# Language-model layer on one core: the value products of a query block in two calls of two heads each

## The chip, the core and the metric

The kernel runs on one NeuronCore of a Trainium2 chip. Its engines are TensorE (PE, with weight loads shown as PEld), VectorE (DVE), ScalarE (ACT), GpSimd (POOL) and SyncE (SP), which work side by side and wait for one another on semaphores. The metric is the device time of one execution in microseconds, as the median of several runs; lower is better.

## The reference

A layer of a language model over 2 sequences of 1024 tokens, width 512, all in float32: an embedding (hot tokens from a table, the others from a smaller table times a projection), causal attention with 16 heads of 32 columns, and a mixture of 16 experts, two of them for each token, beside a shared expert. The change touches the attention:

```python
def _L0_attn_ref(x, w_project, w_out):        # x: layernorm of the embedding
    qkv = jnp.einsum('bsd,od->bso', x, w_project)
    ...
    att = jnp.einsum('bhqd,bhkd->bhqk', q, k) / math.sqrt(HEAD_DIM)
    att = jnp.where(causal[None, None, :, :], jnp.float32(-1000000000.0), att)
    att = jax.nn.softmax(att, axis=-1)
    out = jnp.einsum('bhqk,bhkd->bhqd', att, v)
    out = jnp.transpose(out, (0, 2, 1, 3)).reshape(b, s, d)
    return jnp.einsum('bsd,od->bso', out, w_out)
```

The products of `att` with `v` are the value products.

## The kernel before

The program runs the embedding, the attention and the experts one after another. Every engine has its own program, written out by hand in program order; semaphores (`s_...`) tie them together.

The attention works in eight *units* `u`: four groups `g` of four heads (`GH` = 4) times two sequences `b`. A unit has eight *blocks* `i` of 128 query rows, and a block has four *steps*, one for each head, so a unit has 32 steps `n`, with i = n // 4 and head h = n % 4. Block i sees i + 1 key tiles of 128.

For step n the work passes through the engines like this. TensorE makes the scores (`scores`, line 676). VectorE adds the mask and takes the row maximum (line 815). ScalarE takes the exponentials, unnormalised, into `probs` (line 773). TensorE transposes each 128-wide tile of `probs` into PSUM banks 4 and 5 (`turn`, line 686). ScalarE copies the first bank of a head, key tiles 0 to 3, to `probsT` (line 758, semaphore `s_Ca`), and VectorE the second, which blocks 4 to 7 have (line 760, `s_Cd`). When all four heads of a block are copied, TensorE makes the value products (`heads`, line 699): for each key tile j and head h, `v_unit` (128 x 32) stands in the array and `probsT` (128 x 128) moves through it; the result of head h adds up in partitions 32h to 32h + 31 of PSUM bank 6. A transpose of the reciprocal row sums into another part of bank 6 follows (line 702, `z_inv`) and raises `s_PV`. ScalarE copies that (line 780, `z_rows`), and VectorE multiplies bank 6 with it into `attnT` (line 830, `s_AT`), which frees the bank for the next block.

TensorE's queue in step n of a unit is, in this order: the scores of a later step (n + 2 in the first half of a unit, n + 1 in the second), the transposes of step n - 1, in most steps a piece of the projections of the next unit (`fill_piece`, lines 629 and 642), and, in steps with n % 4 == 2, the value products of the block before. That is two steps behind the end of that block: its last head is transposed in step n % 4 == 0 and copied while TensorE is in the step after. In a unit's first block (n = 2) they are those of block 7 of the unit before. The last unit has no projection pieces. Behind it the transposes of its last step, the first tile of the output projection (line 651) and the value products of the last block follow.

ScalarE goes through copy of step n - 2, exponentials of step n, and in steps with n % 4 == 3 the copy to `z_rows`; VectorE through the row maximum of step n, copy of step n - 2, in steps with n % 4 == 0 the reciprocals for `z_inv`, and with n % 4 == 3 the multiplication into `attnT`.

Of the kernel before, what the change touches and what calls it, by code (L numbers as in the profile page):

```python
# [28 lines left out]
GROUPS, GH = HEADS // 4, 4  # L29
ATT_SCALE = float(HD) ** -0.5  # L30
QT = SEQ // P
# [37 lines left out]
def build(nc, a, out):  # L69
    ctx = ExitStack()  # L70
    with ctx:
# [3 lines left out]
        def sem(name):  # L75
            return ctx.enter_context(nc.semaphore(name))
# [18 lines left out]
        def bank(i, n=1):  # L95
            return psum[:, i:i + n, :].rearrange("p a n -> p (a n)")
# [247 lines left out]
        s_AT = sem("attnT_ready")  # L344
# [44 lines left out]
        HEAD = 16  # L389
# [6 lines left out]
        def score_bank(n):  # L396
            return bank(n % 4) if n < NARROW else bank(2 * (n % 2), 2)

        def turned_banks(i):
            return 1 if i < 4 else 2  # L400
# [9 lines left out]
        def bank_no(i, h, k):  # L410
            return banks.index((i, h, k))

        def copies(e, upto):

            return sum(copier(*x) == e for x in banks[:upto])

        def wait_bank_free(pe, u, n):

            m = n - 2
            x = banks[m % UB]  # L420
            v = u if m >= 0 else u - 1
            e = copier(*x)
            pe.wait_ge(s_Ca if e == "act" else s_Cd, HEAD + v * UCOPY[e] + copies(e, m % UB + 1))
# [191 lines left out]
        def fill_piece(pe, u, b, f, k, loads):  # L615

            if k == 0:

                if f >= 4:
                    pe.wait_ge(s_w, loads)  # L620
                copied, count = ((s_fdve, 0), (s_fact, 1), (s_fdve, 1), (s_fact, 2), (s_fdve, 2), (s_fact, 3))[f]
                pe.wait_ge(copied, HEAD + 3 * u + count)
            if f < 4:
                side, half = f % 2, f // 2
                if side == 0:
                    pe.wait_ge(s_wqlo, 4 * (u // 2) + k + 1)
                    pe.wait_ge(s_xplo, 8 * (u - 1) + 4 * half + k + 1)
                for t, (w, x) in enumerate(((wq_hi, x_lo), (wq_hi, x_hi), (wq_lo, x_hi))):
                    mm = pe.matmul(bank(7), w[:, k, side * P:(side + 1) * P], x[:, k, :],  # L629
                                   start=(k == 0 and t == 0), stop=(k == KC - 1 and t == 2), skip_group_check=True)  # L630
                if side == 1 and k < KC - 1:
                    mm.then_inc(s_xpused, 1)
            else:
                mm = value_products(pe, b, f, k)
            if k == KC - 1:
                mm.then_inc(s_fill, 1)

        def value_products(pe, b, f, k):

            t0 = b * SEQ + ((f - 4) * 4 + k) * P  # L640
            for c in range(KC):
                mm = pe.matmul(bank(7)[:, k * P:(k + 1) * P], xnT[:, c, t0:t0 + P],  # L642
                               w_unit[:, c, 2 * P:3 * P], start=(c == 0), stop=(c == KC - 1))
            return mm

        def output_tile(pe, c):

            pe.wait_ge(s_atlo, c + 1)
            for g in range(GROUPS):
                for t, (x, w) in enumerate(((at_hi, wo_hi), (at_lo, wo_hi), (at_hi, wo_lo))):  # L650
                    mm = pe.matmul(bank(c % 2), x[:, c % 2, g * P:(g + 1) * P], w[:, g, :],  # L651
                                   start=(g == 0 and t == 0), stop=(g == GROUPS - 1 and t == 2))
            mm.then_inc(s_op, 1)

        def att_pe(pe):
            def scores(u, b, n):
                i, h = n // GH, n % GH

                if n < 2:
                    pe.wait_ge(s_E, HEAD + u * STEPS - 1)  # L660
                elif n < 4:
                    pe.wait_ge(s_E, HEAD + u * STEPS)
                elif n < NARROW:
                    pe.wait_ge(s_E, HEAD + u * STEPS + n - 3)
                elif n == NARROW:
                    pe.wait_ge(s_E, HEAD + u * STEPS + n - 2)
                else:
                    pe.wait_ge(s_E, HEAD + u * STEPS + n - 1)
                dst = score_bank(n)
                if n == NARROW:  # L670
                    pe.wait_ge(s_high[b], STACKED * (u // 2 + 1))
                qs = q_stack[:, h, i * P:(i + 1) * P]
                for c0, ks in ((0, k_low[b]), (512, k_high))[0:1 if n < NARROW else 2]:

                    c1 = min(max((i + 1) * P, c0 + 256), c0 + 512)
                    mm = pe.matmul(dst[:, c0:c1], qs, ks[:, h, 0:c1 - c0], start=True, stop=True)  # L676
                mm.then_inc(s_S, 1)

            def turn(u, n):
                i, h = n // GH, n % GH  # L680
                pe.wait_ge(s_E, HEAD + u * STEPS + n + 1)
                for k in range(turned_banks(i)):
                    m = bank_no(i, h, k)
                    wait_bank_free(pe, u, m)
                    for j in range(4 * k, min(4 * k + 4, i + 1)):
                        mm = pe.transpose(bank(4 + m % 2)[:, (j - 4 * k) * P:(j - 4 * k + 1) * P],  # L686
                                          probs[n % PSLOTS][:, j * P:(j + 1) * P], ident[:, :])
                    mm.then_inc(s_T, 1)

            def heads(u, b, i):  # L690

                last = bank_no(i, GH - 1, turned_banks(i) - 1) + 1
                for e, s in (("act", s_Ca), ("dve", s_Cd)):
                    pe.wait_ge(s, HEAD + u * UCOPY[e] + copies(e, last))

                pe.wait_ge(s_AT, HEAD + u * QT + i)
                for j in range(i + 1):
                    for h in range(GH):
                        pe.matmul(bank(6)[32 * h:32 * h + 32, 0:P], v_unit[b][:, j, 32 * h:32 * h + 32],  # L699
                                  probsT[i % 2][:, h, j * P:(j + 1) * P], start=(j == 0), stop=(j == i))  # L700
                pe.wait_ge(s_Z, HEAD + u * QT + i + 1)
                pe.transpose(bank(6)[:, P:2 * P], z_inv[:, i % 2, :, :].rearrange("p h d -> p (h d)"),  # L702
                             ident[:, :]).then_inc(s_PV, 1)

            def unit(u, b, g, prev, nxt):

                for n in range(STEPS):
                    if n + 2 < NARROW:
                        scores(u, b, n + 2)
                    elif NARROW <= n + 1 < STEPS:  # L710
                        scores(u, b, n + 1)
                    elif n + 1 == STEPS and nxt:
                        first_scores(u + 1, 1 - b, g + b)
                    if n >= 1:
                        turn(u, n - 1)
                    elif prev:
                        turn(u - 1, STEPS - 1)
                    if nxt and 0 <= (n - 2) // 5 < FILLS and (n - 2) % 5 < KC:
                        fill_piece(pe, u + 1, 1 - b, (n - 2) // 5, (n - 2) % 5, 16 * (g + 1 + b))
                    if n % GH == 2:  # L720
                        if n > GH:
                            heads(u, b, n // GH - 1)
                        elif prev:
                            heads(u - 1, 1 - b, QT - 1)

            def first_scores(u, b, g):

                pe.wait_ge(s_low[b], STACKED * (g + 1))
                pe.wait_ge(s_fact, HEAD + 3 * u + 3)
                pe.wait_ge(s_fdve, HEAD + 3 * u + 3)  # L730
                scores(u, b, 0)
                scores(u, b, 1)

            first_scores(0, 0, 0)
            unit(0, 0, 0, False, True)
            for g in range(GROUPS - 1):
                unit(2 * g + 1, 1, g, True, True)
                unit(2 * g + 2, 0, g + 1, True, True)
            last = 2 * GROUPS - 1
            unit(last, 1, GROUPS - 1, True, False)  # L740
            turn(last, STEPS - 1)
            pe.wait_ge(s_wolo, KC)
            output_tile(pe, 0)
            heads(last, 1, QT - 1)

        def copy_turned(eng, who, u, n):
            i, h = n // GH, n % GH
# [1142 lines left out]
        def _(pe):  # L1890
# [31 lines left out]
            for c in range(NT + 3):  # L1922
# [28 lines left out]
                if c in FIRST_FILL:  # L1951
                    first_piece(pe, c)
            pe.wait_ge(s_xC, NT)
            att_pe(pe)
            moe_pe(pe)

# [48 lines left out]
```

## Time and profile before

| | |
|---|---|
| median of 3 runs | 979.15 us (976.76 to 980.65) |
| the profiled execution | 977.9 us, its span 976.1 us |
| attention stage, about | 118 to 568 us of the span |
| TensorE busy, share of the span | 93% |
| VectorE, ScalarE, GpSimd busy | 67%, 61%, 47% |
| value products (line 699) | 2304 records, 76.2 us busy |

The profile is of one execution. Its page lists busy times of the engines, the granted clock of TensorE by slices, and groups of like instructions. The trace behind the page gives the same for any stretch, and a timeline, in which like neighbours on an engine are merged into one row with a count (x8). A float32 product with 128 columns is two records of TensorE in the profile, each with a weight load of its own. A record's time runs from its start to the modelled end of its results, so records that follow each other closely overlap, and a group's busy time is far below count times mean.

### The profile page before, as it was taken

The numbers are of one execution on the slowest core, as the hardware profiler recorded it, in microseconds if no ns is written. First come the engines' busy times: TensorE is split into PE (matmuls) and PEld (weight loads), VectorE is DVE, ScalarE is ACT, GpSimd is POOL, SyncE is SP. The second block draws the span as 40 slices with busy tenths as digits, with TensorE's granted clock in tenths as the row PEclk, the third lists the DMA queues.
The fourth block names the chain that finished last, engine by engine and source line by source line (L and its number), as shares of the span: only waits on it lengthen the run. The fifth ranks groups of instructions, "written<-read, shape, count | busy, mean of one in ns | idle before, by whom it ended". The sixth has DMA issues, their size and how long they took to land.

```text
span 976.1 us, 21791 instructions
## 1 busy us (share of the span) xinstructions
PE 911.5 (93%) x6891; PEld 696.4 (71%) x6891; DVE 658.1 (67%) x1653; ACT 596.4 (61%) x1306; POOL 455.6 (47%) x489
## 2 busy tenths in 40 slices
PE   6779799999999999999997899899989999999995
PEld 5335578787887878788795678777766766766673
DVE  8885567576666757666675867758866666666662
ACT  6322487776877777687878822231147777777772
POOL 8277554533515255350500316533345477357443
PEclk9799899999999999999999999999999999999998
DMA  6135452423424242342415321171459578736430
GB/s 229 42 99 140 121 121 51 97 58 89 108 58 99 53 118 58 91 96 54 98 43 153 137 109 65 54 291 55 184 146 383 153 126 191 260 68 127 56 49 0
DMA packets 60513, 110.52 MB, mean 113 GB/s; under 512 B 15412, under 2 KB 21556, under 8 KB 58098
## 3 DMA queue, kind: packets, MB, share of 16 engines
q1 hardware_dynamic: 48082, 87.15, 30.0%
q0 software_dynamic: 12320, 21.99, 11.9%
q8 instruction: 57, 0.93, 0.4%
q14 instruction: 54, 0.44, 0.2%
HBM read 53.03 MB, written 25.17 MB: 80 GB/s over the span
## 4 chain that ended last, share of the span: by engine, by line
PE 76%; DVE 8%; issue 7%; ACT 3%; SPq 2%; POOL 2%; DMA 1%; POOLq 0%; DVEq 0%; ACTq 0%
PE psum L1535 13%; PE psum L686 11%; PE psum L1610 8%; PE psum L699 7%; PE psum L629 6%; PE psum L676 6%; PE psum L642 5%; PE psum L651 4%; PE psum L1463 3%; SPq L444 2%; PE psum L1579 2%; DVE psum L815 2%; PE psum L1557 2%; PE psum L608 1%; PE psum L702 1%
## 5 line engine op out<-in xcount | busy, mean ns | idle before, releaser
L773 ACT ACTIVATE probs<-psum,nmax 128x128 f32<-128x128 f32 (+7 forms) x256 | 191.2, 747 | 37.5 <-DVE nmax L815 35.2
L815 DVE CUSTOM_DVE_ANT_0 psum<-psum,mask_row 128x128 f32<-128x128 f32 (+7 forms) x256 | 192.2, 767 | 27.6 <-PE psum L676 25.9
L686 PE MATMUL psum<-ident,probs 128*128 128x128 f32 x1152 | 175.3, 276 | 12.5 <-ACT probs L773 5.5
L686 PEld LDWEIGHTS psum<-ident,probs 128*128 128x128 f32 x1152 | 134.4, 140 | 48.2 <-ACT probs L773 17.9
L758 ACT COPY probsT<-psum 128x512 f32<-128x512 f32 (+3 forms) x256 | 129.1, 504 | 33.6 <-PE psum L686 31.2
L1049 POOL DMA_INDIRECT out<-xnT,slot_out x47 | 88.3, 1879 | 90.0 <-DMA out<-xnT,slot_out 53.2
L481 POOL CAST part_hi<-full 128x512 fp32r<-128x512 f32 x28 | 17.1, 610 | 206.4 <-ACT full L546 160.6
L676 PE MATMUL psum<-k_low,q_stack 128*128 128x512 f32 (+2 forms) x256 | 105.2, 419 | 5.1 <-ACT probs L773 3.3
L830 DVE TENSOR_TENSOR attnT<-psum,z_rows 128x128 f32<-128x128 f32 x64 | 18.7, 292 | 111.5 <-ACT z_rows L780 111.5
L1610 PE MATMUL psum<-w_dn,gated_T 128*128 x188 | 88.6, 593 | 1.0 <-ACT gated_T L1103 1.0
L1388 DVE TENSOR_TENSOR w_lo<-w_gu,w_hi 128x1024 fp32r<-128x1024 f32 x48 | 58.7, 1225 | 41.5 <-ACT w_hi L1132 40.5
L1388 DVE TENSOR_TENSOR ws_lo<-w_gu,ws_hi 128x1024 fp32r<-128x1024 f32 x46 | 56.3, 1225 | 37.5 <-ACT ws_hi L1132 33.8
L699 PE MATMUL psum<-probsT,v_unit 128*32 128x128 f32 x2304 | 76.2, 275 | 0.0
L508 POOL TENSOR_TENSOR x_lo<-xnT,x_hi 128x512 fp32r<-128x512 f32 x56 | 71.8, 1281 | 4.4
L699 PEld LDWEIGHTS psum<-probsT,v_unit 128*32 128x32 f32 x2304 | 59.0, 109 | 15.5 <-ACT probsT L758 7.8
L642 PE MATMUL psum<-w_unit,xnT 128*128 128x128 f32 x512 | 66.8, 275 | 0.2
L760 DVE COPY probsT<-psum 128x128 f32<-128x128 f32 (+3 forms) x128 | 62.2, 486 | 3.9 <-PE psum L686 2.9
L642 PEld LDWEIGHTS psum<-w_unit,xnT 128*128 128x128 f32 x512 | 61.7, 192 | 0.6 <-issue 0.6
L676 PEld LDWEIGHTS psum<-k_low,q_stack 128*128 128x128 f32 x256 | 52.1, 207 | 14.0 <-ACT probs L773 9.7
L1117 ACT ACTIVATE xnT<-psum,slot_w 128x512 f32<-128x512 f32 x47 | 32.3, 688 | 47.7 <-PE psum L1610 47.7
L1132 ACT CAST w_hi<-w_gu 128x1024 fp32r x48 | 50.3, 1049 | 10.3 <-issue 7.8
L629 PE MATMUL psum<-x_lo,wq_hi 128*128 128x512 f32 x112 | 54.3, 485 | 0.0
(273 smaller groups left out, 2143.1 us busy)
## 6 DMA issues: line engine op xcount, KB each, us to landing
w_gu<-in_wgu SPq DMA_DIRECT2D x16, 1024.0 KB, 5.9
q_stack<-part_hi SPq DMA_DIRECT2D x128, 64.0 KB, 2.0
q_stack<-part_lo SPq DMA_DIRECT2D x128, 64.0 KB, 2.0
w_dn<-in_wd SPq DMA_DIRECT2D x16, 512.0 KB, 7.8
out<-acc SPq DMA_DIRECT2D x17, 256.0 KB, 5.9
hot_all<-xn SPq DMA_DIRECT2D x4, 1024.0 KB, 8.0
h_scratch<-hot_all SPq DMA_DIRECT2D x16, 256.0 KB
k_low<-part_hi SPq DMA_DIRECT2D x64, 64.0 KB, 2.0
```

The lines of the kernel that those rows point to most:

```text
L629: mm = pe.matmul(bank(7), w[:, k, side * P:(side + 1) * P], x[:, k, :], start=(k == 0 and t == 0), stop=(k == KC - 1 and t == 2), skip_gro ...
L642: mm = pe.matmul(bank(7)[:, k * P:(k + 1) * P], xnT[:, c, t0:t0 + P], w_unit[:, c, 2 * P:3 * P], start=(c == 0), stop=(c == KC - 1))
L676: mm = pe.matmul(dst[:, c0:c1], qs, ks[:, h, 0:c1 - c0], start=True, stop=True)
L686: mm = pe.transpose(bank(4 + m % 2)[:, (j - 4 * k) * P:(j - 4 * k + 1) * P], probs[n % PSLOTS][:, j * P:(j + 1) * P], ident[:, :])
L699: pe.matmul(bank(6)[32 * h:32 * h + 32, 0:P], v_unit[b][:, j, 32 * h:32 * h + 32], probsT[i % 2][:, h, j * P:(j + 1) * P], start=(j == 0), ...
L758: eng.copy(dst, src).then_inc(s_Ca, 1)
L773: act.activation(probs[n % PSLOTS][:, 0:(i + 1) * P], score_bank(n)[:, 0:(i + 1) * P], ACT.Exp, bias=nmax[:, n % 4:n % 4 + 1], scale=-1.0, ...
L815: dve.tensor_tensor_reduce(out=row, in0=row, in1=mask_row[:, (QT - 1 - i) * P:QT * P], scale=1.0, scalar=3.0e38, op0=ALU.add, op1=ALU.min, ...
L1049: pool.indirect_dma_start(out=out, out_offset=bass.IndirectOffsetOnAxis(ap=slot_out[:, j:j + 1], axis=0), in_=y_rows[j % ROUTED_RING], in_ ...
L1388: dve.tensor_tensor(w_lo[j % 2][:, k, :].rearrange("p k n -> p (k n)"), w_gu[:, bass.ds(slot, 1), k, :].rearrange("p o k n -> p (o k n)"), ...
L1535: mm = pe.matmul(bank(2 + p), x[:, p, k * P:(k + 1) * P], w[p][:, k, :], start=(k == 0 and t == 0), stop=(k == KC - 1 and t == 2), skip_gr ...
L1610: mm = pe.matmul(bank(6 + p), gated_T[:, p, k * P:(k + 1) * P], w_dn[:, bass.ds(half, 1), k, :].rearrange("p o n -> p (o n)"), start=(k == 0),
```

## The change

`heads` gets a fourth argument, `pair`. The call with pair 0 makes the products of heads 0 and 1, the call with pair 1 those of heads 2 and 3 and, as before, the transpose of `z_inv`. Each call waits for the copies up to its own second head: pair 0 for those of head 1, pair 1 for those of head 3. The wait for the normalised block before (`s_AT`) is at pair 0, the wait for the reciprocals (`s_Z`) at pair 1. In a unit pair 0 is called at the end of the steps with n % 4 == 1, pair 1 at the end of those with n % 4 == 2, where all four heads were. Behind the last unit both calls follow each other. The programs of the other engines are the same.

```diff
-            def heads(u, b, i):
-
-                last = bank_no(i, GH - 1, turned_banks(i) - 1) + 1
+            def heads(u, b, i, pair):
+
+                last = bank_no(i, 2 * pair + 1, turned_banks(i) - 1) + 1
                 for e, s in (("act", s_Ca), ("dve", s_Cd)):
                     pe.wait_ge(s, HEAD + u * UCOPY[e] + copies(e, last))
-
-                pe.wait_ge(s_AT, HEAD + u * QT + i)
+                if pair == 0:
+                    pe.wait_ge(s_AT, HEAD + u * QT + i)
                 for j in range(i + 1):
-                    for h in range(GH):
+                    for h in (2 * pair, 2 * pair + 1):
                         pe.matmul(bank(6)[32 * h:32 * h + 32, 0:P], v_unit[b][:, j, 32 * h:32 * h + 32],
                                   probsT[i % 2][:, h, j * P:(j + 1) * P], start=(j == 0), stop=(j == i))
+                if pair == 0:
+                    return
                 pe.wait_ge(s_Z, HEAD + u * QT + i + 1)
...
+                    if n % GH == 1:
+                        if n > GH:
+                            heads(u, b, n // GH - 1, 0)
+                        elif prev:
+                            heads(u - 1, 1 - b, QT - 1, 0)
                     if n % GH == 2:
                         if n > GH:
-                            heads(u, b, n // GH - 1)
+                            heads(u, b, n // GH - 1, 1)
                         elif prev:
-                            heads(u - 1, 1 - b, QT - 1)
+                            heads(u - 1, 1 - b, QT - 1, 1)
...
-            heads(last, 1, QT - 1)
+            heads(last, 1, QT - 1, 0)
+            heads(last, 1, QT - 1, 1)
```

Two places in TensorE's program show it. In these rows a product stands once, with a count behind it (x27), and the semaphores that it waits for in brackets. L676 are scores, L686 transposes of `probs`, L629 and L642 projection pieces, L699 value products, L702 (L704 after the change) the transpose of `z_inv`.

The first place is the end of a unit with projection pieces, steps n = 29 and 30, where the value products of block 6 (seven key tiles) stand. Before:

```order
L676 MATMUL psum<-k_low,q_stack 128x512 [waits probs_ready]
L676 MATMUL psum<-k_high,q_stack 128x512
L686 MATMUL psum<-ident,probs 128x128 [waits probsT_copied_by_act,probs_ready]
L686 MATMUL psum<-ident,probs 128x128 x3
L686 MATMUL psum<-ident,probs 128x128 [waits probsT_copied_by_dve]
L686 MATMUL psum<-ident,probs 128x128 x3
L642 MATMUL psum<-w_unit,xnT 128x128 x4
L699 MATMUL psum<-probsT,v_unit 32x128 [waits attnT_ready,probsT_copied_by_dve,probsT_copied_by_act]
L699 MATMUL psum<-probsT,v_unit 32x128 x27
L702 MATMUL psum<-ident,z_inv 128x128 [waits z_inverse_ready]
```

With the change, from the projection piece of step 29 on:

```order
L642 MATMUL psum<-w_unit,xnT 128x128 x4
L699 MATMUL psum<-probsT,v_unit 32x128 [waits attnT_ready,probsT_copied_by_dve,probsT_copied_by_act]
L699 MATMUL psum<-probsT,v_unit 32x128 x13
L676 MATMUL psum<-k_low,q_stack 128x512 [waits probs_ready]
L676 MATMUL psum<-k_high,q_stack 128x512
L686 MATMUL psum<-ident,probs 128x128 [waits probsT_copied_by_act,probs_ready]
L686 MATMUL psum<-ident,probs 128x128 x3
L686 MATMUL psum<-ident,probs 128x128 [waits probsT_copied_by_dve]
L686 MATMUL psum<-ident,probs 128x128 x3
L642 MATMUL psum<-w_unit,xnT 128x128 x4
L699 MATMUL psum<-probsT,v_unit 32x128 [waits probsT_copied_by_dve,probsT_copied_by_act]
L699 MATMUL psum<-probsT,v_unit 32x128 x13
```

One run of 28 products became two runs of 14, the first of them ahead of the scores and transposes of step 30.

The second place is the start of a unit, steps n = 1 and 2, where the 32 products of block 7 of the unit before stand. Before:

```order
L686 MATMUL psum<-ident,probs 128x128 [waits probsT_copied_by_act,probs_ready]
L676 MATMUL psum<-k_low,q_stack 128x256 [waits probs_ready]
L686 MATMUL psum<-ident,probs 128x128 [waits probsT_copied_by_dve,probs_ready]
L629 MATMUL psum<-x_lo,wq_hi 128x512 [waits projection_rows_low_ready,projection_weights_low_ready,projection_copied_by_dve]
L629 MATMUL psum<-x_hi,wq_hi 128x512
L629 MATMUL psum<-x_hi,wq_lo 128x512
L699 MATMUL psum<-probsT,v_unit 32x128 [waits attnT_ready,probsT_copied_by_dve,probsT_copied_by_act]
L699 MATMUL psum<-probsT,v_unit 32x128 x31
L702 MATMUL psum<-ident,z_inv 128x128 [waits z_inverse_ready]
```

With the change:

```order
L686 MATMUL psum<-ident,probs 128x128 [waits probsT_copied_by_act,probs_ready]
L699 MATMUL psum<-probsT,v_unit 32x128 [waits attnT_ready,probsT_copied_by_dve,probsT_copied_by_act]
L699 MATMUL psum<-probsT,v_unit 32x128 x15
L676 MATMUL psum<-k_low,q_stack 128x256 [waits probs_ready]
L686 MATMUL psum<-ident,probs 128x128 [waits probsT_copied_by_dve,probs_ready]
L629 MATMUL psum<-x_lo,wq_hi 128x512 [waits projection_rows_low_ready,projection_weights_low_ready,projection_copied_by_dve]
L629 MATMUL psum<-x_hi,wq_hi 128x512
L629 MATMUL psum<-x_hi,wq_lo 128x512
L699 MATMUL psum<-probsT,v_unit 32x128 [waits probsT_copied_by_dve,probsT_copied_by_act]
L699 MATMUL psum<-probsT,v_unit 32x128 x15
L704 MATMUL psum<-ident,z_inv 128x128 [waits z_inverse_ready]
```

Sixteen products moved ahead of the last score matmul and transpose of step 2.

## Rows read from the trace of the kernel before

**Rows 1.** The page: span, busy time and share of engines, slices.

```profile
span 976.1 us, 21791 instructions
PE 911.5 (93%) x6891; PEld 696.4 (71%) x6891; DVE 658.1 (67%) x1653; ACT 596.4 (61%) x1306; POOL 455.6 (47%) x489
```

**Rows 2.** Busy time of engines in the attention stage (column names ahead).

```profile
core 0: us, PE busy (x) PEld busy (x) DVE busy (x) ACT busy (x) POOL busy (x), PEclk, DMA share, GB/s
118.00:568.00 450.00, 433.54 (x4678) 355.58 (x4677) 296.79 (x836) 338.73 (x836) 171.97 (x196) 1.00 0.35 87
```

**Rows 3.** TensorE's groups of the stage: busy us, mean ns of one | idle before.

```profile
L699 PE MATMUL psum<-probsT,v_unit 128*32 128x128 f32 x2304 | 76.2, 275 | 0.0
L642 PE MATMUL psum<-w_unit,xnT 128*128 128x128 f32 x448 | 59.2, 275 | 0.0
```

**Rows 4.** Timeline of TensorE around bursts: start us, us, engine line, names, shapes, xcount.

```profile
343.13 1.96 PE L699 MATMUL psum<-probsT,v_unit 128*32 128x128 f32 x64
...
347.03 0.28 PE L676 MATMUL psum<-k_low,q_stack 128*128 128x256 f32 x1
347.15 0.38 PE L686 MATMUL psum<-ident,probs 128*128 128x128 f32 x2
347.28 0.48 PE L629 MATMUL psum<-x_lo,wq_hi 128*128 128x512 f32 x1
...
348.07 0.34 PE L676 MATMUL psum<-k_low,q_stack 128*128 128x384 f32 x1
...
348.56 0.43 PE L699 MATMUL psum<-probsT,v_unit 128*32 128x128 f32 x8
...
353.83 0.65 PE L699 MATMUL psum<-probsT,v_unit 128*32 128x128 f32 x16
...
359.73 0.86 PE L699 MATMUL psum<-probsT,v_unit 128*32 128x128 f32 x24
...
366.93 1.08 PE L699 MATMUL psum<-probsT,v_unit 128*32 128x128 f32 x32
```

**Rows 5.** Line 699 in short stretches of one burst; (x) counts those under way.

```profile
core 0: us, PE busy (x) PEld busy (x), PEclk, DMA share, GB/s
343.12:343.15 0.03, 0.02 (x4) 0.02 (x4) 1.00 0.00 0
343.15:343.25 0.10, 0.10 (x4) 0.10 (x8) 1.00 0.65 143
343.25:343.29 0.04, 0.04 (x8) 0.04 (x9) 1.00 0.76 205
343.29:343.36 0.07, 0.07 (x8) 0.07 (x4) 1.00 0.75 176
343.36:343.40 0.04, 0.04 (x12) 0.04 (x8) 1.00 2.21 461
```

**Rows 6.** Timeline of TensorE, steps 23 to 26 of a unit.

```profile
320.14 1.06 PE L642 MATMUL psum<-w_unit,xnT 128*128 128x128 f32 x8
...
321.44 0.82 PE L686 MATMUL psum<-ident,probs 128*128 128x128 f32 x6
322.10 1.06 PE L642 MATMUL psum<-w_unit,xnT 128*128 128x128 f32 x8
...
325.46 0.93 PE L686 MATMUL psum<-ident,probs 128*128 128x128 f32 x7
326.32 1.52 PE L699 MATMUL psum<-probsT,v_unit 128*32 128x128 f32 x48
327.76 0.33 PE L702 MATMUL psum<-ident,z_inv 128*128 128x128 f32 x1
```

**Rows 7.** TensorE's waits, 118 to 568 us: total us, times, longest.

```profile
PE psum L686 <- ACT probs L773: 5.1, 11, 1.1
PE psum L676 <- ACT probs L773: 3.3, 8, 0.7
PE psum L686 <- ACT probsT L758: 3.2, 16, 0.3
PE psum L686 <- DVE probsT L760: 2.6, 14, 0.2
PE psum L676 <- DMA k_high<-part_lo: 0.3, 1, 0.3
```

**Rows 8.** The same, in the last unit, 515 to 567 us.

```profile
PE psum L686 <- ACT probs L773: 3.7, 4, 1.1
...
PE psum L686 <- ACT probsT L758: 0.6, 2, 0.3
```

**Rows 9.** Timeline of TensorE at a unit's start, steps 0 to 2.

```profile
339.59 0.36 PE L676 MATMUL psum<-k_low,q_stack 128*128 128x256 f32 x1
...
340.16 1.11 PE L686 MATMUL psum<-ident,probs 128*128 128x128 f32 x8 [0.21 <-ACT probsT L758]
...
341.56 0.30 PE L686 MATMUL psum<-ident,probs 128*128 128x128 f32 x1 [0.17 <-ACT probsT L758]
...
341.61 0.36 PE L676 MATMUL psum<-k_low,q_stack 128*128 128x256 f32 x1
...
342.15 0.30 PE L686 MATMUL psum<-ident,probs 128*128 128x128 f32 x1 [0.17 <-DVE probsT L760]
```

**Rows 10.** Timeline of ScalarE and VectorE behind the burst at 343.13.

```profile
345.61 0.27 ACT L758 COPY probsT<-psum 128x128 f32<-128x128 f32 x1
...
345.68 0.29 DVE L830 TENSOR_TENSOR attnT<-psum,z_rows 128x128 f32<-128x128 f32 x1 [3.16 <-ACT z_rows L780]
```

## Prediction, made before the changed kernel was timed

> **What bounds the kernel now.** I read the page first. TensorE is busy for 93% of the span, VectorE for 67%, ScalarE for 61% [rows 1], and in the attention stage, from 118 to 568 us, TensorE is busy for 433.5 of 450 us at a granted clock of 1.00 [rows 2]. "Busy" can hide waiting, so I then read TensorE's own waits in that stage: 14.5 us of idle time in 50 waits [rows 7]. A matmul's tail counts as busy, so a wait costs more than its idle time. At 339.59 a score matmul of 256 columns is followed by its transpose 0.57 us later [rows 9], where the same pair at 347.03 is 0.12 us apart [rows 4]: a stall of 0.45 us, listed as 0.21. With 0.24 us more for each of the 50 waits TensorE truly stalls about 14.5 + 12 = 26.5 us. By the same count the last unit, which has no projections to fill the gaps, has 7.6 + 14 x 0.24 = 11 us of it (the rows of [rows 8], and the 8 waits of 3.3 us of [rows 7], all of which lie in it), and each of the seven others 2.2 us. So TensorE's own work sets the stage's time, and whatever TensorE's queue gains or loses there, the span gains or loses, less what falls into those 26.5 us.
>
> **What the value products cost now.** A burst is the products of one query block: with i + 1 key tiles, 4(i+1) products and 8(i+1) records, two of each product. The bursts of 1, 2, 3, 4 and 8 key tiles last 0.43, 0.65, 0.86, 1.08 and 1.96 us [rows 4]: 0.21 us, and (1.96 - 0.43)/7 = 0.218 us for each key tile, that is, for 8 records. A record lasts 0.275 us [rows 3], so many must be under way at once. Rows 5 show how: four records start within 0.03 us, none in the next 0.10 us, then four more, then four more: waves of four, one wave in 0.109 us. What else takes about 0.11 us? A record of a transpose (6 from 321.44 to 322.10) or of a value projection (8 last 1.06 us; less one record's 0.275 us, seven steps of 0.112) [rows 3, 6]. These also have 128 moving float32 columns, but use all 128 columns of the array. So a record that fills a quarter of the array's columns takes as long as one that fills them all, and the four heads' products are cheap because four of them, in the four column strips (heads 0 to 3 write partitions 0, 32, 64 and 96), run side by side.
>
> **The change, part by part.**
>
> 1. *Half the strips stand idle.* Each of the two calls now issues products of two heads only. The same 2304 records run, but in waves of two. If a record's strip is occupied for 0.109 us whatever its neighbours do, each key tile of each pair needs two waves of 0.109 us, so a pair's burst costs 0.218 us for each key tile, as all four heads did before. The eight blocks have 36 key tiles, the eight units 288: 288 x 0.218 = **+63 us**.
>
> The row shows starts 7 ns apart at most and waves 0.109 us apart [rows 5]. The Trainium skill ("TensorE: Matmul & The Clock Gate", Part 3: Packing small matmuls) gives a packed group of tiles the time of one matmul and about 4 ns for each further tile, so a wave of two would be 8 ns shorter than one of four. Over the 1152 waves then run, that would make this term some 9 us smaller (an estimate from that page), 54 us. I stay with the trace: what separates waves there is how long a strip is occupied, not the stagger within a wave.
>
> 2. *64 more bursts.* Going into and out of a burst costs time. From the seven transposes at 325.46 to the transpose of z at 327.76 it takes 2.30 us [rows 6]; 7 x 0.109 and 6 x 0.218 account for 2.07, which leaves 0.23 us for entry and exit. The last block's two bursts stand back to back, so 63 are extra: 63 x 0.23 = **+14.5 us**. Bounds: 0 if leaving towards a score matmul is free, 0.23 as seen.
>
> 3. *The moved half.* Pair 0's burst stands one step earlier, behind that step's transposes and projection piece, with the score matmuls of step n%4 == 2 queued behind it. It waits for the copies of heads 0 and 1 and for the normalised previous block. At 348.56 a burst of block 0 starts; its pair 0 would start near 348.07, behind the piece at 347.28 to 348.07 [rows 4]. The normalisation that it needs ends at 345.97 and an even later copy than it needs at 345.88 [rows 10]: two microseconds to spare. So the new waits cost 0. The old wait, for head 3's copies, stays with pair 1, at the same place; burst entries look alike with and without a piece ahead of them, so I give it no gain.
>
> 4. *What falls into stalls.* The new burst in step 1 of a unit stands just ahead of the stall at 342.15 (0.53 us behind its score matmul) [rows 9], and covers it; that is about 3 us over the units. Elsewhere a longer step 1 and 2 gives ScalarE and VectorE, 338.7 and 296.8 us busy in 450 [rows 2], time to catch up, but a stall in steps 3 and 0 is set by the exponentials of that very step. In the last unit a block gets 0.45 to 2 us more TensorE work against 1.4 us of stalls. Bounds: 3 us and all 26.5 us. I take **-12 us**, nearer to the first, since most stalls are not next to the new work.
>
> 5. ScalarE, VectorE, GpSimd and SyncE keep their programs. The transpose of z, on which ScalarE and then VectorE wait, still follows the last product. The experts' stage comes after and only shifts.
>
> Sum: 63 + 14.5 - 12 = +65.5 us. The profiled span of 976.1 us becomes about 1041.5. The profiled run took 977.9 us and the median is 979.15, so I put the change on the median: **1044.5 us**.
>
> **The rivals.**
>
> *A, the forecast.* A strip is occupied for 0.109 us for each record. For it: the equality with full-width records [rows 6].
>
> *B, the overlap isn't between heads.* Two records belong to each product and stand next to each other in the program. If a wave is both records of two heads, not one of four, then a pair's waves are as full as before, and halves cost the same as the whole. The product term is then 0 and the sum 14.5 - 12 = +2.5 us: 981.6 us, between 974 and 990 by the bounds of terms 2 and 4. Against it: one strip would have to run two records at once, which makes it twice as fast as the array runs a full-width record. For it there is the Trainium skill, in the same Part 3: matmuls start and end strictly in program order, and only weight loads move ahead. By that rule a wave is the two records of two neighbouring products, and the time would be this rival's. The rows cannot say which records form a wave.
>
> *C, faster.* As B, and the half moved into step 1 fills stalls for what it is worth: in the unit's first steps and in the last unit all 26.5 us go, against 14.5 us of entries: -12 us, 967 us. It decides only if the products stay at 0.027 us for each record; any loss of overlap above a fifth (12 of 63 us) turns it round.
>
> *D, slower than A.* Pair 0's wait holds up TensorE's queue in step 1, and the score matmuls behind it reach VectorE late, so the chain of scores, maximum, exponentials and transposes stalls in every block. At 0.35 us in each of 64 blocks that is +22 us, 1066 us. Against it are the two spare microseconds of part 3.
>
> **How the numbers follow.** A 0.84, B 0.09, C 0.03, D 0.04. A's bounds: 63 + 14.5 - 26.5 = +51 gives 1030, 63 + 14.5 - 3 = +74.5 gives 1054; the runs shown spread by 4 us, and term 2's lower bound and the new waits add a few more. 1026 to 1060 holds nearly all of A and leaves out B, C and D, some 0.17 with A's edges. About 0.5%, 5 us, is what a measurement of this kernel can tell from no change. Faster than that: C, 0.03. Within it: half of B, 0.05. Slower: A, D and the rest of B, 0.92.
>
> **What the changed profile would show.** Under A: the value products' group stays at 2304 records of 0.275 us, but its busy time goes from 76.2 to about 150 us; a burst with half the records lasts as long as the whole one did (1.96 us for 32 records); waves of two, 0.109 us apart. TensorE's idle time in the stage falls from 14.5 us to under 10; the stage, 450 us now, takes about 515; the experts' stage is as long as before. Entries: a product starts 0.2 us behind the transpose ahead of it in 64 more places. Under B a burst of 32 records lasts some 1.1 us. Under D the value products or the score matmuls behind them show waits for the normalisation or for copies. The forecast is wrong if the burst's slope for a key tile and pair is nearer to 0.109 than to 0.218 us, or if the 26.5 us of stalls all vanish.

## Result

The changed kernel takes 1045.6 us (median of 4 runs, 1044.3 to 1046.6), the kernel before 978.0 us beside it. The ratio is 1.068, with a 95% interval of 1.066 to 1.070: 67.7 us slower, where 65.5 were forecast. The page of its profiled execution, with the lines that answer to [rows 1]:

```profile
span 1043.5 us, 21855 instructions
PE 984.0 (94%) x6891; PEld 755.6 (72%) x6891; DVE 655.1 (63%) x1653; ACT 602.7 (58%) x1306; POOL 452.9 (43%) x489
```

TensorE runs the same 6891 matmuls and is busy for 72.5 us more. The other engines do the same work over a longer span. The time went into one group, which answers to [rows 3]:

```profile
L699 PE MATMUL psum<-probsT,v_unit 128*32 128x128 f32 x2304 | 150.0, 275 | 0.0
```

The same 2304 value-product records with the same mean of 275 ns were 76.2 us busy before: each takes as long as it did, but only half as many lie side by side. The timeline shows it burst by burst. First the two bursts of a block with eight key tiles, then those of a block with one (columns as in [rows 4]):

```profile
309.04 1.94 PE L699 MATMUL psum<-probsT,v_unit 128*32 128x128 f32 x32
310.91 0.39 PE L676 MATMUL psum<-k_low,q_stack 128*128 128x256 f32 x1
311.13 0.27 PE L686 MATMUL psum<-ident,probs 128*128 128x128 f32 x1
...
312.04 1.94 PE L699 MATMUL psum<-probsT,v_unit 128*32 128x128 f32 x32
313.91 0.33 PE L704 MATMUL psum<-ident,z_inv 128*128 128x128 f32 x1
...
317.05 0.41 PE L699 MATMUL psum<-probsT,v_unit 128*32 128x128 f32 x4
...
317.99 0.41 PE L699 MATMUL psum<-probsT,v_unit 128*32 128x128 f32 x4
```

32 records now last 1.94 us, as long as the 64 records of the whole block did (1.96 us) [rows 4]. Cut into short stretches, as in [rows 5], the waves have two records where they had four, at the same distance:

```profile
core 0: us, PE busy (x) PEld busy (x), PEclk, DMA share, GB/s
312.03:312.06 0.03, 0.03 (x2) 0.03 (x2) 1.00 0.02 0
312.06:312.16 0.10, 0.10 (x2) 0.10 (x4) 1.00 0.00 0
312.16:312.19 0.03, 0.03 (x4) 0.03 (x4) 1.00 0.00 0
312.19:312.27 0.08, 0.08 (x4) 0.08 (x2) 1.00 0.00 0
312.27:312.30 0.03, 0.03 (x6) 0.03 (x4) 1.00 0.00 0
```

The (x) counts records under way: 2, then 4, then 6, where [rows 5] has 4, 8, 12.

TensorE's waits over the attention stage, the answer to [rows 7], are fewer:

```profile
PE psum L686 <- ACT probsT L766: 3.3, 16, 0.3
PE psum L686 <- ACT probs L781: 3.1, 3, 1.1
PE psum L676 <- ACT probs L781: 2.0, 4, 0.9
PE psum L686 <- DVE probsT L768: 1.3, 7, 0.2
```

That is 9.7 us in 30 waits, against 14.5 us in 50 [rows 7]. No line is a value product: the new waits, for the copies of heads 0 and 1 and for the normalised block, hold nothing up. The experts' stage only shifted. From the last value product to the end it is 408.5 us before and 408.9 us after, with TensorE busy for 387 us in both.

The sum can be checked against the trace itself. Take all distances from one matmul's start to the next one's, from the first value product to the last, and add them up by the kinds of the two neighbours:

| neighbours | before, us | after, us | difference |
|---|---|---|---|
| product, product | 58.7 | 115.4 | +56.7 |
| into a burst (from another matmul to a product) | 16.3 | 32.6 | +16.3 |
| out of a burst | 12.8 | 25.6 | +12.8 |
| neighbours that a new burst now parts | 31.7 | 20.2 | -11.5 |
| all others | 329.2 | 322.8 | -6.4 |
| sum | 448.7 | 516.6 | +67.9 |

The first three rows are 85.8 us. 63 of them are the added waves, which leaves 22.8 us. Some 7.3 us of the fourth row are ordinary distances, which TensorE would also pay without a stall (27 times about 0.235 us behind a projection piece of 512 columns, and 34 small ones of 0.03 us). So going into and out of 63 more bursts costs 22.8 - 7.3 = 15.5 us net, 0.25 us each. The rest of rows four and five, 4.2 + 6.4 = 10.6 us, are stalls that vanished. If each distance is compared with the usual one of the same two neighbours, about 5 us of them vanished in the last unit and 0.8 us in each of the seven others.

### The profile page after: what moved, and what is told of

Read it like the earlier page. It is cut to its first block, busy times and chain, and to the rows that moved or that the text cites. A ratio compares the mean times of both kernels' runs of the same rounds, so it can differ in the third digit from the quotient of the medians.

```text
span 1043.5 us, 21855 instructions
## 1 busy us (share of the span) xinstructions
PE 984.0 (94%) x6891; PEld 755.6 (72%) x6891; DVE 655.1 (63%) x1653; ACT 602.7 (58%) x1306; POOL 452.9 (43%) x489
## 4 chain that ended last, share of the span: by engine, by line
PE 82%; DVE 7%; issue 5%; ACT 3%; DMA 1%; POOL 1%; POOLq 0%; DVEq 0%; ACTq 0%
PE psum L699 13%; PE psum L1543 12%; PE psum L686 11%; PE psum L1618 8%; PE psum L629 7%; PE psum L676 7%; PE psum L642 5%; PE psum L651 4%; PE psum L1471 3%; PE psum L1587 2%; PE psum L1565 2%; PE psum L704 2%; PE psum L1554 1%; PE psum L1909 1%; DVE psum L823 1%
## 5 line engine op out<-in xcount | busy, mean ns | idle before, releaser
L686 PE MATMUL psum<-ident,probs 128*128 128x128 f32 x1152 | 172.7, 275 | 9.0 <-ACT probs L781 3.5
L686 PEld LDWEIGHTS psum<-ident,probs 128*128 128x128 f32 x1152 | 136.1, 140 | 35.7 <-issue 9.3
L699 PE MATMUL psum<-probsT,v_unit 128*32 128x128 f32 x2304 | 150.0, 275 | 0.0
L699 PEld LDWEIGHTS psum<-probsT,v_unit 128*32 128x32 f32 x2304 | 115.9, 109 | 30.8 <-issue 14.1
L1057 POOL DMA_INDIRECT out<-xnT,slot_out x47 | 90.9, 1933 | 93.6 <-DMA out<-xnT,slot_out 65.2
L676 PE MATMUL psum<-k_low,q_stack 128*128 128x512 f32 (+2 forms) x256 | 108.0, 430 | 3.5 <-ACT probs L781 2.0
L642 PE MATMUL psum<-w_unit,xnT 128*128 128x128 f32 x512 | 66.8, 275 | 0.2
L676 PEld LDWEIGHTS psum<-k_low,q_stack 128*128 128x128 f32 x256 | 51.9, 206 | 19.9 <-issue 9.3
L642 PEld LDWEIGHTS psum<-w_unit,xnT 128*128 128x128 f32 x512 | 61.7, 192 | 0.6 <-issue 0.6
L629 PE MATMUL psum<-x_lo,wq_hi 128*128 128x512 f32 x112 | 54.6, 487 | 0.0
```

Of the source, the lines that this page charges most:

```text
L1057: pool.indirect_dma_start(out=out, out_offset=bass.IndirectOffsetOnAxis(ap=slot_out[:, j:j + 1], axis=0), in_=y_rows[j % ROUTED_RING], in_ ...
```

## Experiments

All ratios are to runs of the kernel before on the same chip (977.6 to 979.1 us).

### Is it the missing strips, or the place and the cutting?

**e1, both pairs in the old place.** The changed kernel with

```diff
-                    if n % GH == 1:
-                        if n > GH:
-                            heads(u, b, n // GH - 1, 0)
...
                     if n % GH == 2:
-                        if n > GH:
-                            heads(u, b, n // GH - 1, 1)
...
+                        for pair in range(2):
+                            if n > GH:
+                                heads(u, b, n // GH - 1, pair)
...
```

> The changed kernel, but with both calls at the end of step n%4 == 2, one behind the other, where all four heads stood before the change. Theory 'strips' (a record holds its column strip for 0.109 us, and two strips idle while a pair runs): most of the cost stays. In the changed kernel the last block has its two calls back to back, and its 64 records take 3.29 us, against 1.96 us with four heads mixed: 1.33 us more, where twice 8 x 0.218 would be 1.74 more, so some 0.41 us of the second pair overlaps the first. For k key tiles 0.218k - 0.41 us more, not below zero: 4.8 us for a unit's blocks, 38 us for eight units, less 5 to 12 us that falls into stalls: 1008 us (1002 to 1016). Rival 'place' (the cost is the first pair's earlier place and its waits): back near the kernel before, 978 to 983 us.

Measured: 1014.3 us, ratio 1.036 (1.033 to 1.040). Half of the loss stays though nothing stands in another place and no burst is added. What changed is the order of the products within one burst, with the wait for head 3's copies now in its middle. The page's line and the bursts of one, two, three and eight key tiles:

```profile
L699 PE MATMUL psum<-probsT,v_unit 128*32 128x128 f32 x2304 | 114.1, 275 | 0.0
```

```profile
360.30 3.29 PE L699 MATMUL psum<-probsT,v_unit 128*32 128x128 f32 x64
367.08 0.43 PE L699 MATMUL psum<-probsT,v_unit 128*32 128x128 f32 x8
372.35 0.66 PE L699 MATMUL psum<-probsT,v_unit 128*32 128x128 f32 x16
378.26 1.10 PE L699 MATMUL psum<-probsT,v_unit 128*32 128x128 f32 x24
```

The small bursts are as short as with four heads mixed (0.43 and 0.65 us) [rows 4], so there TensorE fills its idle strips with products from further down its queue. From three key tiles on it no longer can: 1.10 against 0.86 us, and 3.29 against 1.96. The group is 37.9 us busier than before and the kernel 36.7 us slower: nearly nothing of it fell into stalls.

**e3, one head for each call.** Four calls with the head `h` as the argument: in step 1 head 0 between the score matmuls and the transposes and head 1 at the end, in step 2 heads 2 and 3 in the same way.

```diff
-                for j in range(i + 1):
-                    for h in range(GH):
-                        pe.matmul(bank(6)[32 * h:32 * h + 32, 0:P], v_unit[b][:, j, 32 * h:32 * h + 32],
+                for j in range(i + 1):
+                    pe.matmul(bank(6)[32 * h:32 * h + 32, 0:P], v_unit[b][:, j, 32 * h:32 * h + 32],
...
```

> The dose doubled: one head for each call. In step n%4 == 1 head 0 stands between the score matmuls and the transposes and head 1 at the end of the step, in step n%4 == 2 heads 2 and 3 in the same way. 'Strips': only one strip of four is busy, so each key tile costs 4 x 0.218 us, 3 x 63 = 189 us more than in the kernel before, and 3 x 63 more entries at 0.23 us are 43 us; up to 26 us fall into stalls: about 1190 us (1175 to 1215). Rival 'place or bursts': the cost of a cut is about the same for each further cut, 67 us for one more burst of a block, 3 x 67 = 201 us: 1179 us, but then with bursts whose records follow each other as closely as before; under 'strips' the 16 records of a head and 8 key tiles take 1.9 us.

Measured: 1187.3 us, ratio 1.212 (1.208 to 1.216), 209.7 us slower.

```profile
L698 PE MATMUL psum<-probsT,v_unit 128*32 128x128 f32 x2304 | 293.0, 275 | 0.2 <-DVE attnT L838 0.2
```

The same 2304 records are now 293 us busy: 76, 150 and 293 us with four, two and one strip at work. The four bursts of a block with eight key tiles, in this kernel's timeline:

```profile
442.46 1.93 PE L698 MATMUL psum<-probsT,v_unit 128*32 128x128 f32 x16
444.59 1.94 PE L698 MATMUL psum<-probsT,v_unit 128*32 128x128 f32 x16
446.77 1.93 PE L698 MATMUL psum<-probsT,v_unit 128*32 128x128 f32 x16
449.59 1.93 PE L698 MATMUL psum<-probsT,v_unit 128*32 128x128 f32 x16
```

16 records of one head take as long as 32 of two or 64 of four: waves of one, again 0.109 us apart. So a strip takes one record at a time, and not the two records of a product at once, as rival B had it. The rival, a fixed price for each cut, comes near in the total but would have left the records as close together as before.

### What does a cut cost when the strips stay full?

**e2, cut by key tiles.** The kernel before, all four heads in both parts, the second part one step later:

```diff
-            def heads(u, b, i):
+            def heads(u, b, i, part):
+                cut = (i + 1) // 2
...
-                for j in range(i + 1):
+                for j in (range(cut), range(cut, i + 1))[part]:
...
-                    if n % GH == 2:
+                    if n % GH >= 2:
...
```

> The kernel before, with its burst cut in two by key tiles instead of by heads: all four heads' products of the first half of the key tiles in step n%4 == 2, those of the second half and the transpose of z_inv in step n%4 == 3. As many bursts as in the changed kernel (less those of block 0, whose first half is empty), but every wave has four heads. 'Strips': only entry and exit of 55 more bursts, 0.23 us each, 12.6 us, less what falls into stalls: 978 to 991 us, most likely 985. Rival 'bursts' (it is being cut in two that costs): near the changed kernel's 1046 us.

Measured: 1071.7 us, ratio 1.094 (1.091 to 1.098). That was a bad miss of 87 us. The products were not it, since their group is 87.8 us busy, which is 76.2 and a tail of 0.21 us for each of 55 more bursts. TensorE had got new waits:

```profile
PE psum L686 <- ACT probs L777: 20.8, 32, 1.4
PE psum L686 <- ACT probsT L762: 19.6, 33, 1.0
PE psum L676 <- ACT probs L777: 16.3, 19, 1.6
PE psum L686 <- DVE probsT L764: 14.1, 33, 0.7
```

The edit had changed two things: besides the cut, the end of the burst, which raises `s_PV`, also came a step later.

**e5, one burst, one step later.** To tell the two apart, the kernel before with nothing cut:

```diff
-                    if n % GH == 2:
+                    if n % GH == 3:
...
```

> The kernel before with the whole burst of four heads and the transpose of z_inv in step n%4 == 3 instead of 2; nothing is cut. e2 took 1071.7 us where 985 were expected, with 71 us of idle TensorE time ahead of transposes and scores, so either its extra bursts or its place costs that. Theory 'place of the end': the burst's end raises s_PV late, and ScalarE, whose queue has the copy to z_rows next in step 3, waits there and is late with its copies and exponentials: 1055 to 1065 us here too. Rival 'bursts': one uncut burst costs nothing wherever it stands: 975 to 985 us.

Measured: 1061.6 us, ratio 1.085 (1.083 to 1.087), as expected of the place. ScalarE's waits in e5 (total us, times, longest):

```profile
ACT z_rows L780 <- PE psum L702: 130.8, 62, 3.5
```

The same line in the kernel before:

```profile
ACT z_rows L780 <- PE psum L702: 39.4, 52, 2.1
```

ScalarE's queue has the copy to `z_rows` in step 3 and, behind it, the copy that frees a PSUM bank for TensorE's next transposes. If TensorE raises `s_PV` only at the end of its own step 3, the two engines wait for each other in turn. That reading fits the waits on `probs` and `probsT` in e2 and e5, and one round of it stands in e5's timeline:

```profile
356.68 0.33 PE L702 MATMUL psum<-ident,z_inv 128*128 128x128 f32 x1
357.05 0.27 ACT L780 COPY z_rows<-psum 128x128 f32<-128x128 f32 x1 [2.80 <-PE psum L702]
357.21 0.59 ACT L758 COPY probsT<-psum 128x512 f32<-128x512 f32 x1
357.94 0.63 PE L686 MATMUL psum<-ident,probs 128*128 128x128 f32 x4 [0.53 <-ACT probsT L758]
```

ScalarE waits 2.80 us for the transpose behind the burst, only then copies to `probsT`, and TensorE waits for that copy. No run took the loop apart. The difference between e2 and e5, 94.16 - 82.54 = 11.6 us for 55 bursts or 0.21 us each, is then an estimate of the cut alone. It is a small difference of two large ones, good to some 4 us, and e2 has less work left in step 3 than e5. The busy time of the products, 87.8 - 76.2 = 11.6 us, says the same.

**e4 and e4b, the burst made twice, without and with something between.** The first adds full waves at one place and nothing else; the second (its edit shown as added lines only) moves the transpose of `z_inv` from behind the two passes to between them.

```diff
-                for j in range(i + 1):
+                for j in 2 * list(range(i + 1)):
```

```diff
+                for once in range(2):
+                    for j in range(i + 1):
...
+                    if once == 0:
+                        pe.wait_ge(s_Z, HEAD + u * QT + i + 1)
+                        pe.transpose(bank(6)[:, P:2 * P], z_inv[:, i % 2, :, :].rearrange("p h d -> p (h d)"),
+                                     ident[:, :])
+                mm.then_inc(s_PV, 1)
```

> The kernel before, with the value products of each block made twice, one pass behind the other, all four heads mixed (the second pass starts the sums again, so the result is the same). It adds 288 x 0.218 = 63 us to TensorE's queue at one place, with no new entries, no new waits and no idle strips. It measures the share that falls into stalls: 978 + 63 = 1041 us with none of it, 1015 us with all 26.5 us of them; the prediction's 12 us give 1029. If the time is above 1045, other engines get a new wait from the longer step 2.

> The products made twice, as in e4_products_twice, but with the transpose of z_inv between the two passes instead of behind them; the last product raises the semaphore that the transpose raised. Against e4 (1035.5 us) each of 64 blocks goes out of the narrow products and into them once more, in the same step, with full waves and no other moved work. It is the price of entry and exit alone: 64 x 0.23 = 14.7 us, less up to 5 us of stalls: 1048 us (1045 to 1051). If entry and exit cost nothing, 1035.

Measured: e4 1035.5 us, ratio 1.058 (1.054 to 1.061); e4b 1055.3 us, ratio 1.078 (1.075 to 1.080). e4 adds 57.9 us where its products add 63, so about 5 us fell into stalls, fewer than the 12 of the prediction. The step from e4 to e4b is 19.8 us, 0.31 us for each of 64 partings, where 14.7 us were expected. (By each one's own runs of the kernel before it is 18.3 us, 0.29 each.) In e4b both sides of the parting are the transpose of `z_inv`, and the product behind it starts 0.26 us after it, where it starts 0.20 us after a transpose of `probs`:

```profile
326.59 0.65 PE L700 MATMUL psum<-probsT,v_unit 128*32 128x128 f32 x16
327.16 0.33 PE L704 MATMUL psum<-ident,z_inv 128*128 128x128 f32 x1
327.42 0.64 PE L700 MATMUL psum<-probsT,v_unit 128*32 128x128 f32 x16
```

So about 0.3 us is the price next to that transpose, and 0.21 to 0.25 elsewhere.

### Does the first pair's place matter?

**e8, pair 0 in step 2.** The changed kernel, pair 0's call moved from the end of step 1 to between the score matmuls and the transposes of step 2:

```diff
                         first_scores(u + 1, 1 - b, g + b)
+                    if n % GH == 2:
+                        if n > GH:
+                            heads(u, b, n // GH - 1, 0)
...
                     if n >= 1:
...
-                    if n % GH == 1:
-                        if n > GH:
-                            heads(u, b, n // GH - 1, 0)
...
```

> The changed kernel with pair 0's burst one step later than the change puts it: in step n%4 == 2, between the score matmuls and the transposes, so that it stays apart from pair 1's at the step's end. Same waves, same number of bursts, another place for half the products. The entry price is now taken from e4b: (1055.3 - 1035.5)/64 = 0.31 us, so the changed kernel's sum reads 63 + 63 x 0.31 = 82.5 us of TensorE work, of which 67.7 were seen. Theory 'two places fill stalls' (spreading the work over two steps is why 15 us vanish, where e4, with all of it in one step, lost 5 us): here 82.5 - 5 = 77 us, 1055 us (1050 to 1060). Rival 'the first pair's place does nothing': as the changed kernel, 1046 us.

Measured: 1045.0 us, ratio 1.067 (1.065 to 1.069), the same as the changed kernel within 1 us. The expectation missed by 10 us, and e4b's 0.31 us for every burst is only a part of that. The sum of distances, made as for the changed kernel, has about 13 us for entries and exits in e8, 0.21 us each, and 8 to 9 us of vanished stalls, where the expectation had 19.5 and 5. The place of the first pair is neither a gain nor a loss.

**e9, the whole burst earlier.** Since later is dear, is earlier cheap? The kernel before with the burst ahead of the projection piece of its step:

```diff
+                    if n % GH == 2:
+                        if n > GH:
+                            heads(u, b, n // GH - 1)
...
                     if nxt and 0 <= (n - 2) // 5 < FILLS and (n - 2) % 5 < KC:
                         fill_piece(pe, u + 1, 1 - b, (n - 2) // 5, (n - 2) % 5, 16 * (g + 1 + b))
-                    if n % GH == 2:
-                        if n > GH:
-                            heads(u, b, n // GH - 1)
...
```

> The kernel before, with the burst of four heads and the transpose of z_inv ahead of the projection piece of their step instead of behind it, so that s_PV rises up to 0.9 us earlier. e5 showed that one step later costs 83 us. If the stalls in the kernel before come from the burst ending late, this is faster: up to 10 us of the stalls, 970 us. If they come from the exponentials alone, the only change is that head 3's copy, which ended 0.1 to 1.1 us ahead of the burst, is now waited for in most blocks, and TensorE's pieces no longer cover it: 0.3 us in two thirds of 64 blocks, 13 us, 990 us. I expect 985 us (975 to 995).

Measured: 987.3 us, ratio 1.010 (1.007 to 1.012), a small loss of 8.7 us and near the expected 985, though for another reason than the one I gave. The waits for copies to `probsT` are as before (16 and 14 of them, 3.3 and 2.6 us). A new wait stands in TensorE's list:

```profile
PE psum L676 <- DVE v_unit L559: 6.9, 7, 1.0
```

The last projection piece of a unit, now behind the burst, is copied out later, and the next unit's first scores wait for that copy, once in each of seven units. The old place, behind the piece, was the best of the three tried.

### How far ahead does TensorE look?

e1 showed small bursts at full speed though their heads were not mixed. Two more orders of the products within the old burst:

```diff
-                for j in range(i + 1):
-                    for h in range(GH):
+                for j0 in range(0, i + 1, m):
+                    for h in range(GH):
+                        for j in range(j0, min(j0 + m, i + 1)):
```

with m = 2 (e6) and m = 8 (e7).

> The kernel before, with the products of a burst in another order: two key tiles of head 0, the same two of head 1, 2, 3, then the next two key tiles. A strip now has four records behind each other in the program. In the changed kernel's last block the second pair's first products started while eight records of the first pair were still to end, so TensorE looks some eight records ahead. If so, about half to three quarters of the strips stay busy: 20 to 60 us more, 1000 to 1040 us. If TensorE ran its products strictly in order: each wave at most two records, 150 us more or worse. If it looks ahead without a bound: 978 us.

> The same with all key tiles of head 0 first, then of head 1, 2 and 3, in one burst and one place. With a look-ahead of eight records only the seams between heads overlap: a burst of 8 key tiles takes 64 x 0.109 - 3 x 0.4 = 5.8 us instead of 1.96, and the small blocks less in proportion: for k key tiles 0.872k - 1.2 against 0.218k, summed over the eight blocks about 14.5 us, times eight units 116 us, less a few us of stalls: 1085 us (1065 to 1110). With unbounded look-ahead: 978 us.

Measured: e6 980.7 us, ratio 1.001 (1.000 to 1.003), no difference that the runs can tell; e7 1090.4 us, ratio 1.114 (1.112 to 1.117). e6 missed its 20 to 60 us. From e6's timeline, then from e7's:

```profile
359.99 0.88 PE L700 MATMUL psum<-probsT,v_unit 128*32 128x128 f32 x24
367.21 1.12 PE L700 MATMUL psum<-probsT,v_unit 128*32 128x128 f32 x32
```

```profile
395.52 5.95 PE L700 MATMUL psum<-probsT,v_unit 128*32 128x128 f32 x64
404.97 0.43 PE L700 MATMUL psum<-probsT,v_unit 128*32 128x128 f32 x8
410.25 0.66 PE L700 MATMUL psum<-probsT,v_unit 128*32 128x128 f32 x16
416.15 1.59 PE L700 MATMUL psum<-probsT,v_unit 128*32 128x128 f32 x24
```

Up to two key tiles, four records in a row for one strip, the burst costs what it did (0.66 us for 16 records). With three key tiles, six in a row, it jumps from 0.86 to 1.59 us. In e7's longest burst 64 records one by one would take 64 x 0.109 + 0.21 = 7.19 us; it takes 5.95, so each of the three seams between heads saves 0.41 us, nearly four records. Both fit one reading: TensorE passes over about three records that wait for a busy strip, with a fourth under way in it, and starts the next strip's; one more record for the busy strip holds it up. The records under way in that longest burst, ahead of its first seam and in it, show it directly:

```profile
core 0: us, PE busy (x) PEld busy (x), PEclk, DMA share, GB/s
396.76:396.84 0.08, 0.08 (x3) 0.08 (x1) 1.00 0.68 154
397.12:397.17 0.05, 0.05 (x6) 0.05 (x2) 1.00 0.22 42
```

In the trace its first twelve records start singly, nearly all 0.109 us apart. The next four, by their count the last of head 0, each have a second one starting within 0.03 us, the first four of head 1. The limit is for each strip. In e1's longest burst the seam between the pairs saves 0.41 us too (3.29 us against 32 waves and a tail, 3.70), and there each of those nearly four waves is two records of the first pair. The expectation of e6 read this as eight records in all, and so missed.

## Why the prediction was right

*What bounds the kernel.* Right. The work added to TensorE's queue came out in the span nearly one to one, in the changed kernel and in e1, e3 and e4.

*Term 1, idle strips, +63 us.* Right in kind and size. The slope of a pair's burst, (1.94 - 0.41)/7 = 0.219 us for each key tile, is that of four heads before, and the dose of e3 rules out anything but the number of strips at work. Rival B is refuted by the bursts of 32 records, 1.94 us where it had 1.1. The forecast left one thing unsaid. The two records of a product stand next to each other in the program, so waves of one record from each of four heads need records to start ahead of earlier ones; e1, e6 and e7 show that they do, between strips. The Trainium skill ("TensorE: Matmul & The Clock Gate", Part 3: Packing small matmuls) has matmuls start strictly in program order, on which B rested; here the measurement decides. The Trainium skill's 4 ns for each further tile, in the same part, would have made waves of two 8 ns shorter, by the prediction's estimate. Measured, they are 0.109 us apart, like waves of four.

*Term 2, entries and exits, +14.5 us.* Right: 15.5 us from the table, 0.25 us each against the 0.23 read from one burst. e8 and e2 less e5 give 0.21, e4b about 0.3 next to the transpose of `z_inv`.

*Term 3, the new waits, 0.* Right. No value product waits in the list of waits, and e8 shows that the place of pair 0 makes no difference. Rival D, which needed a wait there, is refuted.

*Term 4, what falls into stalls, -12 us.* Right in sum, 10.6 us in the table and 4.8 us of it in the listed idle time; the prediction's 0.24 us for each of the 20 waits that are gone is another 4.8. The stall at 342.15 is covered as forecast: behind the new burst the transpose at 311.13 follows its score matmul by 0.22 us, where it took 0.54. It was the softest term, and its size was in part luck: e1 got back 1 us of 38 and e4 5 of 63, so how much falls into stalls depends on where the work stands, and the bounds (3 to 26.5) were honest. Its being 1.4 us too large and term 2's being 1.0 us too small add up to the 2 us or so by which the forecast was low. That the added waves stand in two steps rather than one may be why the changed kernel got back more than e4; e8, with both bursts in one step but apart, got back 8 to 9 us, so the parting by other work seems to be most of it. No run isolates it.

*Rival C* could not decide once B was out. It also assumed that stalls can be filled at will; e9 and e5, which move the burst either way, were both slower.

## What to carry to other kernels

In this kernel, matmuls that use a quarter of TensorE's columns are only cheap if those for all four strips stand close together in its queue: keep the strips in the innermost loop (at most four records in a row for one strip cost next to nothing here), and before cutting such a group count how many strips each part still has. A record that takes 0.109 us alone costs 0.027 us in company, so a cut by heads doubled the time of the same work. And when a burst is moved, ask who waits for its end: here one step later cost 83 us without a single instruction added.

## What the runs showed of the hardware

TensorE does not start narrow matmuls strictly in program order. Records for an idle strip start ahead of earlier ones that wait for a busy strip, over about three of them for each busy strip (e6, no loss with four records in a row for a strip; e7 and e1, 0.41 us saved at each seam). In the changed kernel's last block, where the two calls stand back to back behind different waits, it does so across the semaphore wait between them, for copies that had ended 1.9 us before the burst began:

```profile
631.55 3.29 PE L699 MATMUL psum<-probsT,v_unit 128*32 128x128 f32 x64
```

3.29 us for 64 records, where two bursts of 32 take 1.94 us each. e1 has such a seam in each of its 64 blocks.

Going from full-width matmuls to quarter-width ones and back costs 0.21 us for a burst in e8 and in e2 less e5, 0.25 us in the changed kernel, and about 0.3 us where the transpose of `z_inv`, 128 float32 columns, stands between two bursts (e4b).
